# A decoder layer with eight routed experts on one core: new step lists for four engines, a new order of SyncE's last transfers, the slot table moved up, and TensorE's fifteen tiles written out

## The reference, cut to what matters

```
x = x + gated_memory(layernorm(x))        # three 256x256 projections, a decaying sum along the sequence, one more
x = x + softmax(layernorm_J(mix of context and x))
x = x + ffn(layernorm(x), ...)

# ffn
expert_idx = argmax(x @ router_w);  score = sigmoid(max(x @ router_w))
out[row]   = down_w[e] applied to silu(xs @ gate_w[e]) * (xs @ up_w[e]),   e = expert_idx[row], xs = x * score
shared     = silu(x @ shared_gate_w) * (x @ shared_up_w) @ shared_down_w
return out + shared
```

## Time and profile before

| what | us |
|---|---|
| median of 3 runs | 152.68 |
| profiled execution, its own time | 153.2 |
| its span, first to last instruction | 151.4 |
| TensorE busy | 116.8 |
| VectorE busy | 92.8 |
| GpSimd busy | 88.0 |

### The profile page before, as it was taken

The page is one execution under the profiler, slowest core; times in us unless marked ns, Lnnn a source line. Parts: engine busy times, 40 slices in busy tenths (PEclk is TensorE's granted clock), DMA queues, the critical chain, the costliest instruction groups (busy, mean ns, idle before and its releaser), DMA issues.

```text
span 151.4 us, 2634 instructions
## 1 busy us (share of the span) xinstructions
PE 116.8 (77%) x679; PEld 93.2 (62%) x680; DVE 92.8 (61%) x284; ACT 64.2 (42%) x156; POOL 88.0 (58%) x137
## 2 busy tenths in 40 slices
PE   0299999999886989768989703999999939969700
PEld 0187798977683667556879401788868628748400
DVE  2644498579999999989464470267447246174410
ACT  3346879756778179370811001143144042142100
POOL 5224298946668668748785900256657717737550
PEclk9999999999999999999999995599999999999975
DMA  4997624442231500894044806534332411201000
GB/s 141 215 292 166 233 74 142 135 141 71 74 71 51 157 0 4 266 366 142 0 143 163 285 33 185 175 89 131 88 107 62 160 52 47 87 2 44 28 0 0
DMA packets 18204, 17.48 MB, mean 116 GB/s; under 512 B 4108, under 2 KB 17424, under 8 KB 18192
## 3 DMA queue, kind: packets, MB, share of 16 engines
q1 hardware_dynamic: 15792, 13.56, 30.2%
q0 software_dynamic: 1824, 3.22, 6.7%
q10 hardware_dynamic: 576, 0.56, 1.1%
HBM read 13.78 MB, written 5.38 MB: 127 GB/s over the span
## 4 chain that ended last, share of the span: by engine, by line
PE 49%; DVE 19%; issue 9%; POOL 8%; DMA 5%; another core or an unknown queue 3%; ACT 2%; SPq 1%; POOLq 0%; ACTq 0%; DVEq 0%
PE bG L889 12%; PE bQ L889 10%; PE bV L1096 5%; PE bO L1096 3%; DMA ez<-in_ctx_dram 3%; PE bV L889 3%; POOL x_sorted L427 3%; DVE bn L667 3%; PE bV L1045 3%; PE bO L970 2%; POOL rstd L404 2%; PE bT L1067 2%; DVE res L750 2%; DVE z L738 2%
## 5 line engine op out<-in xcount | busy, mean ns | idle before, releaser
L449 POOL DMA_INDIRECT tq<-base_rows,tid x15 | 15.4, 1027 | 15.9 <-DMA base_rows<-res 10.2
L454 POOL DMA_INDIRECT out_dram<-z,tid x15 | 15.2, 1015 | 13.2 <-DVE z L854 4.8
L434 POOL TENSOR_TENSOR gu_lo<-stage,gu_hi 128x512 fp32r<-128x512 f32 x16 | 20.4, 1289 | 2.2 <-ACT gu_hi L499 2.1
L475 ACT ACTIVATE xn<-res,shift,rstd 128x256 f32<-128x256 f32 x22 | 12.0, 596 | 6.0 <-POOL shift L408 5.8
L427 POOL DMA_INDIRECT x_sorted<-xs,dest x8 | 8.5, 1060 | 5.8 <-DVE dest L781 3.6
L404 POOL TENSOR_TENSOR rstd<-vareps,expo 128x2 f32<-128x2 f32 x16 | 11.6, 725 | 0.4
L400 POOL TENSOR_SCALAR vareps<-mv 128x2 f32<-128x2 f32 x16 | 3.6, 225 | 13.1 <-DVE mv L670 12.4
L667 DVE BATCH_NORM_STATS2 bn<-res 128x6 f32<-128x256 f32 x24 | 8.9, 414 | 3.1 <-DMA res<-in_x_dram 3.1
L840 DVE SCALAR_TENSOR_TENSOR tg<-tg,bG 128x256 f32<-128x256 f32 x8 | 3.4, 420 | 10.8 <-ACT tg L622 8.5
L499 ACT CAST gu_hi<-stage 128x512 fp32r<-128x512 f32 x16 | 9.7, 618 | 0.0
L616 ACT CAST xT_hi<-bT 128x256 fp32r<-128x256 f32 x8 | 3.0, 375 | 15.7 <-PE bT L1067 13.7
(11 more groups left out here) (186 smaller groups left out, 354.5 us busy)
## 6 DMA issues: line engine op xcount, KB each, us to landing
stage<-in_L_ffn_gate_w_dram SPq DMA_DIRECT2D x8, 256.0 KB, 2.7
stage<-in_L_ffn_up_w_dram SPq DMA_DIRECT2D x8, 256.0 KB, 2.7
dn<-in_L_ffn_down_w_dram SPq DMA_DIRECT2D x8, 256.0 KB
xs<-x_sorted SPq DMA_DIRECT2D x15, 136.0 KB
res<-in_x_dram SPq DMA_DIRECT2D x4, 256.0 KB, 3.5
base_rows<-res SPq DMA_DIRECT2D x4, 256.0 KB, 2.7
x_sorted<-pad SPq DMA_DIRECT2D x5, 136.0 KB
x_sorted<-pad ACTq DMA_DIRECT2D x4, 136.0 KB
```

The source lines that it names most:

```text
L434: g.tensor_tensor(units[n][2], stage[:, n % RING], f32(units[n][1]), ALU.subtract).then_inc(unit_lo, 1)
L449: g.indirect_dma_start(rb[:, s % TILE_RING, :], None, base_rows, bass.IndirectOffsetOnAxis(tid[:, s:s + 1], 0), bounds_check=N - 1, oob_is ...
L454: g.indirect_dma_start(out_rows, bass.IndirectOffsetOnAxis(tid[:, s:s + 1], 0), ry[:, s % 2, :], None, bounds_check=N - 1, oob_is_err=Fals ...
L475: last = a.activation(dst[:, i, :], res[:, b * TB + i, :], ACT.Identity, bias=shift[:, kind, b, i:i + 1], scale=rstd[:, kind, b, i:i + 1])
```

## The change

1. The four lists of the front part are replaced by others with the same steps. In GpSimd's list, `weight_lo:16` now stands behind `scatter:3`, with 17 to 20 after it; before, it stood ahead of `scatter:0`. `rstd3:3` moves from behind `scatter:1` to ahead of it.
2. In VectorE's list, `slot_table:3` comes straight behind `destination:3`; `shared_add:2`, `shared_hidden:3` and `shared_add:3` follow it.
3. SyncE no longer stores `base_rows` of sequences 0 and 1 ahead of the padding. All four stores come behind the first four row loads. Nothing else in SyncE's program is changed.
4. TensorE's tiles are all written out. The 15 expert numbers are read into registers once, right behind the wait for the table.

```
 POOL_ORDER = """
...
-    rstd2:2 sim_rstd:1 rstd3:0 weight_lo:13 weight_lo:14 weight_lo:15 rstd3:1 rstd2:3 sim_rstd:2
-    scale_rows:0 weight_lo:16 scatter:0 rstd3:2 sim_rstd:3 scale_rows:1 scatter:1 rstd3:3
-    weight_lo:17 scale_rows:2 scatter:2 scale_rows:3 scatter:3 weight_lo:18 weight_lo:19
-    weight_lo:20
+    rstd1:0 rstd1:1 rstd1:2 rstd1:3 rstd2:0 weight_lo:3 weight_lo:4 weight_lo:5 weight_lo:6 rstd2:1
+    weight_lo:7 sim_rstd:0 weight_lo:8 weight_lo:9 weight_lo:10 rstd2:2 rstd3:0 sim_rstd:1
+    weight_lo:11 weight_lo:12 rstd2:3 weight_lo:13 sim_rstd:2 rstd3:1 weight_lo:14 scale_rows:0
+    sim_rstd:3 rstd3:2 weight_lo:15 scatter:0 scale_rows:1 rstd3:3 scatter:1 scale_rows:2 scatter:2
+    scale_rows:3 scatter:3 weight_lo:16 weight_lo:17 weight_lo:18 weight_lo:19 weight_lo:20
...
 DVE_ORDER = """
...
-    destination:2 turned3_lo:3 shared_hidden:2 shared_add:0 route:3 destination:3 shared_add:1
-    shared_hidden:3 shared_add:2 shared_add:3 slot_table:3
...
+    destination:2 turned3_lo:3 shared_add:1 route:3 shared_hidden:2 destination:3 slot_table:3
+    shared_add:2 shared_hidden:3 shared_add:3
...
 PE_ORDER = """
...
-    router:3 router_turn:3 shared_gate:3 rank:3 shared_down:1 shared_up:3 shared_down:2
-    shared_down:3
...
+    router:3 router_turn:3 shared_up:2 rank:3 shared_down:2 shared_gate:3 shared_up:3 shared_down:3
...
 ACT_ORDER = """
...
-    score_tanh:1 norm3:2 turned3_hi:2 softmax_exp:3 router_copy:2 norm3:3 score_tanh:2 weight_hi:19
-    turned3_hi:3 shared_tanh:2 weight_hi:20 router_copy:3 score_tanh:3 shared_tanh:3
...
+    turned3_hi:2 shared_tanh:1 router_copy:2 norm3:3 turned3_hi:3 score_tanh:2 shared_tanh:2
+    weight_hi:17 weight_hi:18 router_copy:3 score_tanh:3 weight_hi:19 shared_tanh:3 weight_hi:20
...
@@ -335,9 +333,6 @@
-            for b in range(B - 2):
-                store_base(b)
-
             sp.wait_ge(pad_made, 1)
...
@@ -359,7 +354,7 @@
             for q in range(TILE_RING):
                 load_rows(q, row[q])
-            for b in range(B - 2, B):
+            for b in range(B):
                 store_base(b)
...
@@ -1097,41 +1092,25 @@
             pe.wait_ge(table_made, 1)
+            e = experts(0, NS)
             pe.wait_ge(unit_lo, len(units) - PROJ)
...
-            e = experts(0, PEEL + 2)
...
-            for s in range(PEEL):
-                hidden_turn(s, s % 2, s >= 2)
+            for s in range(NS + 1):
+                if s < NS:
+                    hidden_turn(s, s % 2, s >= 2)
                 if s >= 1:
-                    down(s - 1, (s - 1) % 2, e[s - 1], False)
...
-            with pe.Fori(0, ROUNDS) as i:
-                e = experts(i * TILE_RING + (PEEL - 1), TILE_RING + 3)
...
-            e = experts(REST - 1, NS - REST + 1)
...
+                    down(s - 1, (s - 1) % 2, e[s - 1], s >= 3)
```

More of the change, by code:

```diff
@@ L34 @@
 PE_ORDER = """
-    turn1:0 turn_ctx:0 turn_ctx:1 gate:0 turn_wk:0 query:0 kv:0 turn1:1 kv:1 value:0 gate:1 query:1
+    turn1:0 turn_ctx:0 turn_ctx:1 turn_wk:0 query:0 gate:0 kv:0 turn1:1 value:0 kv:1 gate:1 query:1
     turn1:2 recall:0 turn_kv:0 value:1 query:2 gate:2 recall:1 turn2:0 value:2 context_mix:0 turn1:3
-    similarity:0 turn2:1 recall:2 context_mix:1 similarity:1 gate:3 query:3 turn2:2 value:3 turn3:0
-    context_mix:2 recall:3 similarity:2 router:0 router_turn:0 shared_gate:0 rank:0 turn3:1 turn2:3
@@ L39 @@
-    shared_up:0 context_mix:3 router:1 similarity:3 router_turn:1 shared_gate:1 turn3:2 rank:1
-    shared_up:1 router:2 router_turn:2 shared_down:0 shared_gate:2 rank:2 turn3:3 shared_up:2
-    router:3 router_turn:3 shared_gate:3 rank:3 shared_down:1 shared_up:3 shared_down:2
-    shared_down:3
+    similarity:0 turn2:1 recall:2 context_mix:1 gate:3 value:3 query:3 similarity:1 turn2:2 recall:3
+    context_mix:2 turn3:0 similarity:2 router:0 shared_gate:0 turn2:3 router_turn:0 context_mix:3
@@ L43 @@
+    shared_up:0 similarity:3 rank:0 shared_down:0 turn3:1 router:1 router_turn:1 shared_gate:1
+    rank:1 turn3:2 shared_up:1 router:2 router_turn:2 shared_gate:2 rank:2 turn3:3 shared_down:1
+    router:3 router_turn:3 shared_up:2 rank:3 shared_down:2 shared_gate:3 shared_up:3 shared_down:3
 """.split()
 ACT_ORDER = """
-    weight_hi:0 weight_hi:1 turned1_hi:0 turned_ctx:0 turned_ctx:1 turned_wk:0 weight_hi:2 norm1:1
-    gate_tanh:0 turned1_hi:1 query_tanh:0 weight_hi:3 weight_hi:4 kv_bias:0 norm1:2 weight_hi:5
@@ L54 @@
-    score_tanh:1 norm3:2 turned3_hi:2 softmax_exp:3 router_copy:2 norm3:3 score_tanh:2 weight_hi:19
-    turned3_hi:3 shared_tanh:2 weight_hi:20 router_copy:3 score_tanh:3 shared_tanh:3
+    weight_hi:0 weight_hi:1 turned1_hi:0 turned_wk:0 turned_ctx:0 turned_ctx:1 weight_hi:2 norm1:1
+    turned1_hi:1 gate_tanh:0 weight_hi:3 query_tanh:0 kv_bias:0 norm1:2 kv_bias:1 weight_hi:4
+    query_tanh:1 turned1_hi:2 turned_kv:0 gate_tanh:1 norm2:0 weight_hi:5 norm1:3 weight_hi:6
+    gate_tanh:2 turned2:0 query_tanh:2 mixed:0 weight_hi:7 norm2:1 turned1_hi:3 weight_hi:8
@@ L60 @@
     stats1:3 memory:0 turned1_lo:2 residual2:0 memory:1 residual2:1 memory:2 sim_stats:0
[L61 to L64, removed]
-    destination:2 turned3_lo:3 shared_hidden:2 shared_add:0 route:3 destination:3 shared_add:1
-    shared_hidden:3 shared_add:2 shared_add:3 slot_table:3
+    sim_centre:0 turned1_lo:3 sim_scale:0 residual2:2 residual3:0 memory:3 sim_stats:1 sim_centre:1
+    sim_scale:1 residual2:3 turned3_lo:0 sim_stats:2 residual3:1 sim_centre:2 route:0 sim_scale:2
+    shared_hidden:0 sim_stats:3 residual3:2 sim_centre:3 turned3_lo:1 sim_scale:3 destination:0
+    route:1 residual3:3 turned3_lo:2 shared_add:0 shared_hidden:1 destination:1 route:2
+    destination:2 turned3_lo:3 shared_add:1 route:3 shared_hidden:2 destination:3 slot_table:3
+    shared_add:2 shared_hidden:3 shared_add:3
 """.split()
 POOL_ORDER = """
-    rstd1:0 rstd1:1 rstd1:2 weight_lo:3 rstd1:3 weight_lo:4 weight_lo:5 weight_lo:6 weight_lo:7
-    rstd2:0 weight_lo:8 weight_lo:9 rstd2:1 weight_lo:10 sim_rstd:0 weight_lo:11 weight_lo:12
-    rstd2:2 sim_rstd:1 rstd3:0 weight_lo:13 weight_lo:14 weight_lo:15 rstd3:1 rstd2:3 sim_rstd:2
-    scale_rows:0 weight_lo:16 scatter:0 rstd3:2 sim_rstd:3 scale_rows:1 scatter:1 rstd3:3
-    weight_lo:17 scale_rows:2 scatter:2 scale_rows:3 scatter:3 weight_lo:18 weight_lo:19
-    weight_lo:20
+    rstd1:0 rstd1:1 rstd1:2 rstd1:3 rstd2:0 weight_lo:3 weight_lo:4 weight_lo:5 weight_lo:6 rstd2:1
[3 more added lines that the diff above has]
+    scale_rows:3 scatter:3 weight_lo:16 weight_lo:17 weight_lo:18 weight_lo:19 weight_lo:20
 """.split()
```

26 lines of the change are left out of this document (5 added, 21 removed).

## The result

| | before | changed |
|---|---|---|
| median | 153.31 us (152.44 to 154.26, 4 runs) | 161.99 us (161.74 to 162.47, 4 runs) |
| profiled execution | 153.2 us | 162.47 us |
| its span | 151.4 us | 160.5 us |

The changed kernel is slower: ratio 1.0568, 95% interval [1.0488, 1.0649]. The kernel before has one run more here than the three shown ahead of the prediction. Some runs of a kernel fall into a slower state; medians and ranges in this document are over all runs, ratios over the fast ones alone.

A forecast was written before the change was run, and what follows sets the result against it. Rows wait for the latest of table, padding and scatters; the change makes padding last. Rows +6.2 us and written-out TensorE -0.3 give +5.9, so 158.6 us against 152.68; range 153.5 to 163.0, the forecast's own 157 to 160.5.

The forecast's parts named there:

- third rival (the late base rows): Gathers behind the row loads start 3 us later than forecast and GpSimd never catches up: 161.6 us, chance 0.10.
- The mechanism: SyncE's list is held at unit 20 until weight_lo:16, with dn and padding behind it: rows issued 6.2 us later.
- End of `scatter:3`: GpSimd's last scatter ends at 83.5, from a hand walk of the new lists; wrong if outside 82 to 85.
- `weight_lo:16`, unit 20, `dn`, the paddings: GpSimd and SyncE steps behind the last scatter: last padding issued at 94.4.
- Landing: Paddings landed at 97.1 by the data in front, chosen over 96.4 by issue alone; rows at about 97.2.
- The table early, worth 0: VectorE's slot table ready at 83.1, 7.3 us earlier, but worth 0 because the padding is now last.
- fourth rival (the early table wins, 147.9): SyncE is through with dn before the scatters, so rows go out at about 86.5: 147.9 us, chance 0.04.
- Base stores, worth 0: Moving two of SyncE's stores from ahead of the padding gains nothing; gathers start 7.7 us behind row loads, hidden.
- The last shared matmul at 87.2: TensorE's last shared matmul ends at 87.2 against 86.99 before, long before the rows.
- TensorE written out, -0.3: TensorE's tiles without the loop save 0.3 us, bounds 0 and -0.6.
- first rival: ScalarE's unexplained waits in the tile part vanish with TensorE's loop: 152.6 us, no change, chance 0.10.
- second rival (a shorter front part): New lists fill VectorE's holes, scatter:3 ends up to 7.6 us earlier; at 4 us, 154.6 us; chance 0.08.

The follow-up runs named there:

- e4: Kernel before with weight_lo:16 moved behind scatter:3 in GpSimd's list (17 behind it, ScalarE's weight_hi:20 at its list's end): 161.36 us, ratio 1.059.
- e1: Changed kernel with weight_lo:16 moved from behind scatter:3 to between rstd3:3 and scatter:1 in GpSimd's list: 156.41 us, ratio 1.0254.
- e2: Changed kernel with SyncE's eight dn loads moved ahead of its load of unit 20: 157.17 us, ratio 1.0299.
- e6: e1 with GpSimd also waiting for the table ahead of weight_lo:17: 156.18 us, ratio 1.0173.
- e7: Changed kernel with only GpSimd waiting for the table ahead of weight_lo:16: 163.59 us, ratio 1.0652.
- e3: Changed kernel with the four old lists, only slot_table:3 moved behind destination:3; new store order and written-out TensorE stay: 154.9 us, ratio 1.0059.
- e9: Changed kernel with base stores of sequences 0 and 1 back ahead of the padding: 164.13 us, ratio 1.0664.
- e8: Changed kernel with TensorE's tiles in the old loop again: 162.48 us, ratio 1.0617.
- e10: Changed kernel with router_copy:1 moved ahead of norm3:2 in ScalarE's list: 162.64 us, ratio 1.0583.
- e5: e3 with GpSimd also waiting for the table ahead of weight_lo:18: 150.11 us, ratio 0.9808.
- e11: Kernel before with slot_table:3 straight behind destination:3 and GpSimd waiting for the table ahead of weight_lo:18; old store order and TensorE loop: 152.88 us, ratio 0.9976.

## Why the prediction was right, and where its terms were off

The forecast was 158.6 us, and slower; it came out slower, at 161.99, inside the range of 153.5 to 163.0 and outside the forecast's own 157 to 160.5. The number lies next to the 161.6 of the third rival (the late base rows), but the gathers start 7.7 us behind the row loads, as in the forecast, so it is not that rival that came true. Step by step:

- **The mechanism** (unit 20 behind `weight_lo:16`, `dn` and the padding behind unit 20, the rows behind the padding): right. The chain of the profile after goes through it, `e4` makes the whole slowdown with it alone, and `e1` and `e2`, which each break one link, take about half of it back (to 156.41 and 157.17, ratios 1.0254 and 1.0299 instead of 1.0568).
- **End of `scatter:3`:** this term was mis-sized. I had 83.5, from a walk that put the last destination at 80.35; measured 82.89 and 86.01, so 2.5 us more, outside the 82 to 85 that I had set as the mark against this step. The walk used step lengths of the old trace, with TensorE at full clock. In the new order the clock falls to half, `shared_gate:1` takes 2.90 us, and `turn3:2`, which stands behind it in TensorE's list, comes late, and with it the routing of the last two sequences: 1.3 to 1.4 us by `e6` against `e1`. Another 0.9 us lies between TensorE's last counting matmuls and VectorE, with no cause shown. That the bound of 3.8 us covered the 2.5 was luck: it was worked out from GpSimd's low parts, and not from TensorE. `e4`, with the old lists, has its last scatter done by 82.92, in time with the earlier trace rows.
- **`weight_lo:16`, unit 20, `dn`, the paddings:** from the end of the scatters to the last padding's issue I had 94.4 - 83.5 = 10.9 us; measured 95.52 - 86.01 = 9.5. The eight `dn` took 4.05 us instead of 4.90 and the padding with its reads 1.22 instead of 1.81. This and the landing, 1.6 us longer than I had it behind the last padding's issue, nearly cancel.
- **Landing:** I chose the estimate by the data in front (12.2 us from unit 20 to the landing) over the one by issue alone (at most 2 us behind the last padding). Measured: 99.80 - 87.39 = 12.4 us, 4.3 behind the last padding's issue. The choice was right, and `e2` bears it out: without the weights in front the rows go out 1.8 us behind the last padding's issue. In the changed kernel they go out 4.45 us behind the last padding's issue, past the 4 us that I had set as the mark against this step: the issue had become 1.4 us faster and the data had not, so the mark should have counted from unit 20.
- **The table early, worth 0:** the value was right (in `e7` the table is ready 5 us earlier still, and nothing is gained), the reason not whole. I had it ready at 83.1; it was ready at 91.0, held by GpSimd. Had the padding been in time, as in `e1`, the table would have been last again. So my fourth rival (the early table wins, 147.9) was priced too well: without GpSimd's wait `e3` shows 154.9 (ratio 1.0059).
- **Base stores, worth 0:** the gathers start 107.64 - 99.97 = 7.7 us behind the row loads, as forecast. The first result write comes 14.6 us behind, not 13.2, and the tile part is as long as before. But "gains nothing, since SyncE is held at unit 20" was wrong: the stores would have run behind unit 20 in the same chain, and `e9` prices them at 1.3 us there. My sum had left them out, so the total did not suffer.
- **The last shared matmul at 87.2:** wrong by 9.6 us. It began at 93.02, took 3.75 us and ended at 96.77, held by VectorE. It stayed hidden, since the rows were issued 3.2 us later still. TensorE therefore rested 5.44 us ahead of the first tile, and not the 11 to 12 that I had named as a sign of being right.
- **TensorE written out, -0.3:** nothing that can be told (`e8`). ScalarE's waits without a releaser are still there, so the first rival fell:

```profile
ACT tg L617 <- remote: 6.0, 2, 4.1
```

The second rival (a shorter front part) fell too: the front part became longer. The sum for the profiled execution was +5.9 us and measured +9.3: of the 3.4 between them 2.5 are the late scatters, 0.3 the other terms of the hand-over, 0.4 the tiles (0.1 longer where I had -0.3), and 0.2 lie outside the span.

## What to carry to other kernels

In an engine's in-order list, a step's price is what stands behind whoever waits for it: `weight_lo:16` costs 1.3 us and its new place cost 8 to 9 (`e4`), through a staging buffer and SyncE's list. Before a step list is taken over, follow each step that frees a ring buffer to the transfer that it frees, and on to everything behind that transfer in its queue. And when an edit makes one of several late things early (the table), look whether the second late one is worth moving too: here the early table gained nothing alone, and about 2% with the stores moved and a wait that keeps GpSimd off VectorE.

## What the runs showed of the hardware

A VectorE instruction with two SBUF operands of 15 numbers took 4.36, 5.57, 5.58 and 5.59 us where GpSimd began a run of successive 128x512 subtractions 0.6 us behind its start (`e3`, `e1`, `e2`, the changed kernel; 5.56 and 5.57 in `e9` and `e10`), and 0.15 us where GpSimd waited for it (`e5`, `e6`, `e7`). Two operands are not what it takes: in `e8` the held instruction reads one (5.64 us, from 0.70 us ahead of the run to its end), though the same instruction, 0.71 us ahead of the run in the changed kernel, took 0.16. In `e4` another instruction with two, the scan, started beside the last subtraction of a run and took 1.27 us, until the run ended at 89.09:

```profile
87.86 1.27 DVE L795 TENSOR_TENSOR_SCAN incl<-one_e,ntile 1x8 f32<-1x8 f32 x1
```

The changed kernel's run is of five, with durations (shortest, median, longest, in ns) and first and last start in the view of its line:

```profile
L429 POOL TENSOR_TENSOR gu_lo<-stage,gu_hi x5: 1262/1263/1280, 86.0 to 91.0; 128x512 fp32r<-128x512 f32 x5
```

VectorE's instruction there ends at 91.00, where the fifth starts; in `e1`, `e2` and `e3` it ends with the run of four, four and three. So in these runs VectorE was let in neither between the first and the second subtraction nor between the next ones, up to the end or the last of the run. The Trainium skill's "SBUF — State Buffer", section "SBUF: two separate sides", says that VectorE and GpSimd share a pair of ports as an exclusive lock, which goes to whoever starts first and is held for the whole instruction, also for VectorE operations with two SBUF inputs against a GpSimd operation that reads SBUF. The runs agree with it that one of the two shuts the other out. They differ in length: one subtraction is 1.26 us, and the wait lasted three or four of them. And by the recorded starts VectorE was first, by 0.6 us, and lost; why stays open. GpSimd's indirect transfer, in the middle of which VectorE's instruction starts, does not do it alone: in `e5` and `e7` it starts at the same place, 0.38 us into the last such transfer, and takes 0.15 us.

The price of TensorE's half clock can be read from the last shared matmul, eight matmuls: 1.97 us behind 1.2 us of rest (`e7`, at 87.88, full clock), 3.56 us behind 3.1 us (`e6`, at 89.22) and 3.75 us behind 6.6 us (the changed kernel, at 93.02). And the same rest can end either way: behind 2.28 us in the front part the clock stayed full in the kernel before and fell to half in `e11`, behind 1.73 and 0.78 us it stayed full in `e6` and fell in `e1`.
